# One layer pair of a graph network: who gathers the rows of eight chunks in each edge phase

## The reference, cut to what matters

```python
h = jnp.maximum(_layernorm(x), 0.0)
x = x + attention(h, edge_index, edge_type_3, node_type_3, ...)
# for each of 3 edge types: a weight per edge, exp(leaky_relu(a_s[src] + a_d[dst]) - max per dst),
#   num = segment_sum(w_edge[:, None] * xw[src], dst);  denom = segment_sum(w_edge, dst)
h = jnp.maximum(_layernorm(x), 0.0)
x = x + convolution(h, edge_index, edge_attr_50, ...)
# filters  = silu(edge_attr @ fW1 + fb1) @ fW2 + fb2
# messages = (x[src] @ dW + db) * filters
# aggregated = segment_sum(messages, dst);  then a two-layer update per node
```

## Time and profile before

| | us |
|---|---|
| median of 3 runs (lowest, highest) | 4208.89 (4204.4, 4209.9) |
| span of the profiled execution | 5383.9 |
| busy in it: TensorE, weight loads, VectorE, ScalarE, GpSimd | 3638.4, 2646.4, 2308.2, 1569.4, 3107.3 |

### The profile page before, as it was taken

The page is one execution under the profiler, slowest core; times in us unless marked ns, Lnnn a source line. Parts: engine busy times, 40 slices in busy tenths (PEclk is TensorE's granted clock), DMA queues, the critical chain, the costliest instruction groups (busy, mean ns, idle before and its releaser), DMA issues. The chain is left out here.

```text
span 5383.9 us, 60755 instructions
## 1 busy us (share of the span) xinstructions
PE 3638.4 (68%) x14213; PEld 2646.4 (49%) x14214; DVE 2308.2 (43%) x5525; ACT 1569.4 (29%) x4773; POOL 3107.3 (58%) x3265
## 2 busy tenths in 40 slices
PE   4666666666666666666756767767676777677768
PEld 2444444444444444444545645555455555555556
DVE  5565666565655565655632222222222222222223
ACT  4454444444444444444510100100000000010001
POOL 5565666555655655555455555555555555555553
PEclk6555555555555555555666666666666666566567
DMA  4121222212211211221222222222222222222222
GB/s 103 43 44 42 44 43 45 44 43 43 44 42 42 45 43 42 44 43 43 53 66 59 57 55 59 55 58 59 55 59 53 60 59 54 58 56 57 59 55 57
DMA packets 163399, 280.57 MB, mean 52 GB/s; under 512 B 80268, under 2 KB 105068, under 8 KB 158793
## 3 DMA queue, kind: packets, MB, share of 16 engines
q0 software_dynamic: 102656, 213.73, 17.0%
q1 hardware_dynamic: 60439, 65.39, 4.4%
q10 hardware_dynamic: 200, 0.48, 0.0%
HBM read 268.31 MB, written 9.73 MB: 52 GB/s over the span
## 5 line engine op out<-in xcount | busy, mean ns | idle before, releaser
L60 POOL DMA_INDIRECT ce_xg<-table,ce_idx x1604 | 1519.4, 947 | 1087.9 <-DVE ce_msg L1537 588.0
L60 POOL DMA_INDIRECT ae_xg<-table,ae_idx x1604 | 1521.4, 949 | 1040.0 <-issue 491.4
L1468 PE MATMUL ce_ps_h<-ce_ea,ce_fw 50*128 50x384 f32 x1076 | 654.7, 749 | 481.2 <-ACT ce_hid L1410 313.5
L1410 ACT ACTIVATE ce_hid<-ce_ps_h,ce_fb 128x768 f32<-128x768 f32 x269 | 242.5, 901 | 2378.1 <-remote 1667.5
L808 PE MATMUL ae_ps_k<-ae_xg,ae_e 128*96 128x129 f32 x3224 | 832.3, 431 | 6.9 <-remote 5.8
L1533 DVE TENSOR_TENSOR ce_ring<-ce_ring,ce_fb 128x768 f32<-128x768 f32 x269 | 259.5, 965 | 1292.0 <-remote 883.0
L1447 PEld LDWEIGHTS ce_ring<-ce_fw,ce_hid 128*128 128x128 f32 x3228 | 621.3, 287 | 359.2 <-issue 342.9
L1447 PE MATMUL ce_ring<-ce_fw,ce_hid 128*128 128x128 f32 x3228 | 708.2, 391 | 110.3 <-issue 109.7
L808 PEld LDWEIGHTS ae_ps_k<-ae_xg,ae_e 128*96 128x96 f32 x3224 | 685.2, 277 | 53.0 <-issue 45.5
L1456 PE MATMUL ce_ring<-ce_hot,ce_msg 128*128 128x32 f32 x3224 | 554.2, 324 | 211.4 <-issue 211.0
L1456 PEld LDWEIGHTS ce_ring<-ce_hot,ce_msg 128*128 128x128 f32 x3224 | 570.1, 264 | 201.9 <-issue 201.3
(11 more groups left out here) (156 smaller groups left out, 3278.6 us busy)
## 6 DMA issues: line engine op xcount, KB each, us to landing
ce_ea<-in_edge_attr SPq DMA_DIRECT2D x90, 450.0 KB
ae_xg<-table,ae_idx POOLq DMA_INDIRECT x1604
ce_xg<-table,ce_idx POOLq DMA_INDIRECT x1604
ae_stage<-table SPq DMA_DIRECT2D x1024, 0.5 KB
ce_stage<-table SPq DMA_DIRECT2D x1024, 0.5 KB
sums<-in_x SPq DMA_DIRECT2D x7, 448.0 KB, 4.2
table<-sums SPq DMA_DIRECT2D x6, 462.0 KB, 3.7
fa_x<-in_x SPq DMA_DIRECT2D x6, 448.0 KB, 6.4
```

Of the source, the lines that this page charges most:

```text
L60: eng.indirect_dma_start(out=out, out_offset=None, in_=table[:, :], in_offset=bass.IndirectOffsetOnAxis(ap=idx, axis=0)).then_inc(done, 16)
L1410: nc.scalar.activation(hid[:, b, :].rearrange("p (k e) -> p k e", k=2), ps_h[:, :].rearrange("p (k e) -> p k e", k=2)[:, :, 0:H], ACT.Silu ...
L1468: last = nc.tensor.matmul(ps_h[:, k * 512:k * 512 + H], fw1[:, :], ea[:, s // LOAD, q:q + H], start=True, stop=True)
```

## The change

In both edge phases SyncE no longer gathers rows. `Carry` is gone, with its two staging tiles, its three semaphores for each phase, the index rows kept in `den`, the turn structure `carry_turns` and the input `src_rows`. GpSimd gathers all six chunks of every full unit (four in the last), 1612 in each phase, and its loop is the same as that of the other engines (`turns`: the first turn, a loop over 43, the last). `load_indices` only loads index lists, and attributes in the convolution. VectorE waits for `gathered[s]` alone.

```diff
-def landed_by(r, i, s, carried=0, j=0):
-    if s != CARRY_SLOT:
-        return r * 16 * CH * (TURNS - 1 if s >= REST else TURNS) + 16 * CH * (i + 1)
-    gathers = CH * TURNS - (CH - REST_CH) - CARRIED
-    if isinstance(carried, int):
-        return r * 16 * gathers + 16 * CH * i + 16 * (chunks_of(i, s) - carried)
-    return r * 16 * gathers + 16 * (SPAN * CH - 1) * carried + 16 * CH * j + 16 * CH
+def landed_by(r, i, s):
+    if s < REST - 1:
+        return r * 16 * CH * TURNS + 16 * CH * (i + 1)
+    if s == REST - 1:
+        return r * 16 * (CH * (TURNS - 1) + REST_CH) + 16 * CH * i + 16 * chunks_of(i, s)
+    return r * 16 * CH * (TURNS - 1) + 16 * CH * (i + 1)
...
-class Carry:
...
 def load_indices(...):
...
-        span(r, 0, 0, True)
-        with sp.Fori(0, CARRIED // 2 - 1) as p:
-            span(r, 2 * p + 1, 1)
-            span(r, 2 * p + 2, 0)
-        span(r, CARRIED - 1, 1)
...
+        with sp.Fori(0, TURNS - 1) as i:
+            for v in range(LOADS):
+                read(r, i, v)
+                sp.dma_start(idx[v][:, :], a["src"][...]).then_inc(idx_in[v], 16)
+                ahead(r, i + 1, v)
...
 def gather_units(...):
...
                 pool.wait_ge(xg_free, r * UNITS + (XS if first else i * SL + s + 1))
                 pool.sem_inc(pool_turn, 1)
-                taken = carried is not None and s == CARRY_SLOT
-                for c in range(CH - 1 if taken else chunks_of(i, s)):
+                for c in range(chunks_of(i, s)):
                     k = s % LOAD * CH + c
                     gather(pool, xg[:, s, c, 0:width], table, idx[s // LOAD][:, k:k + 1], gathered[s])
-        turn(0, True, SL)
-        with pool.Fori(1, SPAN) as i:
-            turn(i, False, SL)
-        with pool.Fori(1, SPANS - 1) as t:
-            turn(SPAN * t, False, SL, t)
-            with pool.Fori(1, SPAN) as j:
-                turn(SPAN * t + j, False, SL)
-        turn(SPAN * CARRIED, False, SL, CARRIED)
-        with pool.Fori(SPAN * CARRIED + 1, TURNS - 1) as i:
-            turn(i, False, SL)
-        turn(TURNS - 1, False, REST)
+        turns(pool, turn)
...
-                def messages(n, s, i, carried, j=0):
+                def messages(n, s, i):
...
-                    carry.landed(dve, r, s, carried)
-                    dve.wait_ge(gathered[s], landed_by(r, i, s, carried, j))
+                    dve.wait_ge(gathered[s], landed_by(r, i, s))
```

More of the change, by code:

```diff
@@ L490, in turns @@
     body(TURNS - 1, False, REST)
[L493 to L497, removed]
 def slot(unit):
@@ L570, in load_indices @@
-def load_indices(nc, sp, a, h, idx, idx_in, gathered, landed, carry, table, xg, xg_free, ahead=lambda r, i, v: None):
+def load_indices(nc, sp, a, h, idx, idx_in, gathered, landed, ahead=lambda r, i, v: None):
     def read(r, i, v, count=SL):
         s = min(v * LOAD + LOAD, count) - 1
[L575 to L605, removed]
@@ L606, in load_indices @@
+        sp.wait_ge(gathered[s], landed_by(r, i, s))
     passes = pass_count(sp, h)
@@ L609, in load_indices @@
             ahead(r, 0, v)
-        span(r, 0, 0, True)
-        with sp.Fori(0, CARRIED // 2 - 1) as p:
-            span(r, 2 * p + 1, 1)
-            span(r, 2 * p + 2, 0)
-        span(r, CARRIED - 1, 1)
[L615 to L619, removed]
+        with sp.Fori(0, TURNS - 1) as i:
+            for v in range(LOADS):
+                read(r, i, v)
+                sp.dma_start(idx[v][:, :],
+                             a["src"][bass.ds((i + 1) * LOADS + v, 1), :, 0:P // 2, :].rearrange("u o p c -> (u o) p c")).then_inc(idx_in[v], 16)
+                ahead(r, i + 1, v)
         for v in range(LOADS):
@@ L624, in load_indices, with gather_units, turn @@
         sp.wait_ge(idx_in[v], 16 * (passes * TURNS + 1))
-    sp.wait_ge(carry.list_in, 16 * (passes * CARRIED + 1))
     sp.sem_inc(landed, 1)
-def gather_units(pool, passes, table, xg, width, idx, idx_in, gathered, xg_free, pool_turn, carry):
+def gather_units(pool, passes, table, xg, width, idx, idx_in, gathered, xg_free, pool_turn):
     with pool.Fori(0, passes) as r:
-        def turn(i, first, count, carried=None):
+        def turn(i, first, count):
             for s in range(count):
@@ L711, in _ @@
             project.load(sp, a)
-            load_indices(nc, sp, a, h, idx, idx_in, gathered, landed, carry, table, xg, s_sum)
+            load_indices(nc, sp, a, h, idx, idx_in, gathered, landed)
             sp.wait_ge(merged, 1)
@@ L720, in _ @@
         def _(pool):
-            gather_units(pool, project.pool_passes, table, xg, ROW, idx, idx_in, gathered, s_sum, pool_turn, carry)
+            gather_units(pool, project.pool_passes, table, xg, ROW, idx, idx_in, gathered, s_sum, pool_turn)
         @block.scalar
@@ L892, in types, with score @@
                                             h.iota[:, 0:NT].unsqueeze(1).to_broadcast([P, CH, NT]), ALU.is_equal).then_inc(s_oh, 1)
-                def score(n, s, i, carried, j):
-                    carry.landed(dve, r, s, carried)
-                    dve.wait_ge(gathered[s], landed_by(r, i, s, carried, j))
+                def score(n, s, i):
+                    dve.wait_ge(gathered[s], landed_by(r, i, s))
                     dve.wait_ge(s_oh, n)
@@ L955, in add_sums, with step @@
                     nc.vector.tensor_tensor(state[64:65, :, win], state[64:65, :, win], kv(ps_a[64:65, KEYS:2 * KEYS]), ALU.add).then_inc(s_den, 1)
-                def step(n, s, i, unit, base, stages, fresh, carried=None, j=0, late=0):
+                def step(n, s, i, unit, base, stages, fresh, late=0):
                     look, chain, weigh, rescaled, merge = (k in stages for k in range(5))
@@ L964, in step @@
                         types(unit)
-                        score(n, s, i, carried, j)
+                        score(n, s, i)
                     if weigh:
@@ L979, in step, with turn @@
                         highest(n - 1, s - 1)
-                def turn(i, first, count, carried, j=0):
+                def turn(i, first, count):
                     back = 0 if first else 4
@@ L985, in turn @@
                         step(r * UNITS + i * SL + s + 1, s, i, i * SL + s, lambda k: base[s + back - k],
-                             [k for k in range(5) if not first or k <= s], first, carried, j)
+                             [k for k in range(5) if not first or k <= s], first)
                 start_pass(nc, dve, h, r, steps, key_ready, begun, project.ring, typ, less_key[:, :, :])
                 dve.wait_ge(project.moved, 16 * (NT + 1))
-                carry_turns(dve, turn)
+                turns(dve, turn)
                 base = bases(nc, mybir.EngineType.DVE, h, UNITS - 4, 4)
@@ L1430, in _ @@
         def _(pool):
[L1431 removed]
+            gather_units(pool, project.pool_passes, table, xg, D, sources.idx, sources.idx_in, gathered, s_msg, pool_turn)
         @block.tensor
@@ L1555, in turn @@
                             one_hot(i * SL + s - 1, v)
-                            messages(n - 1, v, i if s else i - 1, carried, j)
+                            messages(n - 1, v, i if s else i - 1)
                 start_pass(nc, dve, h, r, steps, key_ready, begun, ring)
-                carry_turns(dve, turn)
+                turns(dve, turn)
                 n = (r + 1) * UNITS
@@ L1563, in _ @@
                 one_hot(UNITS - 1, slot(UNITS - 1))
-                messages(n, slot(UNITS - 1), TURNS - 1, CARRIED)
+                messages(n, slot(UNITS - 1), TURNS - 1)
                 for k in range(1, 4):
@@ L1647 @@
     arrays["src"] = np.pad(src.reshape(NU // LOAD, 2, P // 2, LOAD * CH), ((0, 0), (0, 0), (0, 1), (0, 0)))
-    carried = (SPAN * SL * np.arange(1, SPANS) + CARRY_SLOT) * CH + CH - 1
-    arrays["src_rows"] = padded(given["src"], EP, 0).reshape(NU * CH, P)[np.append(carried, carried[0])]
     arrays["dst"] = by_unit(given["dst"], N).transpose(1, 0, 2)
```

18 lines of the change are left out of this document (2 added, 16 removed).

## The result

| | before | changed |
|---|---|---|
| median of 4 runs (lowest, highest), us | 4209.4 (4204.4, 4210.69) | 4227.19 (4226.42, 4230.4) |
| ratio, 95% interval | | 1.0047 (1.0035 to 1.0059) |

By the medians the change costs 17.8 us, 0.42%; the ratio, 0.47%, puts it at 19.8 us (14.7 to 24.8). The forecast was 20.0 us, 0.48%, and 4228.9 us, so the median is 1.7 us under it and inside the range of 4214 to 4236 us.

What follows compares the result with a forecast made beforehand. GpSimd's back-to-back gathers were taken as the bound: 60.5 + 2009.8 + 99.2 + 2005.3 + 36.0 = 4210.8 us against a 4208.9 us median. Adding 20.0 us for 16 gathers to that median gave 4228.9 us, range 4214 to 4236.

Steps and rivals of the forecast that it cites:

- The bound: Both edge phases: GpSimd gathers back to back when timed, with at most some 10 us of waits; rebuilt time 4210.8 us.
- The cause of the stalls: The recorded phases' extra 538.6 and 591.4 us were taken for the cost of recording, absent when timed.
- The price: GpSimd in both phases: 8 more gathers each, one pitch of 1.253 or 1.250 us apiece, 20.0 us slower.
- SyncE's part at nothing: SyncE's row issues, list loads and copies are covered by GpSimd's gathers, so dropping them gives 0.
- VectorE's wait for the staged chunk at nothing: In the 16 carried units this wait ends before the one behind it, so losing it gives 0.
- The room under GpSimd: Compute chains take 6.98 us a unit in attention and 7.20 in convolution, under GpSimd's 7.51.
- Rival A: Compute chains end the phases, so no change: 4208.9 us, chance 0.09; in one phase only, 4218.9 us, chance 0.08.
- the rule beside it: Starting transfers from several engines saves only usually small starting time, so dropping SyncE's chunks costs next to nothing.
- Rival B: SyncE's rows delay index lists; removing 25.4 us of GpSimd's list waits makes it faster, 4203.5 us, chance 0.06.
- Rival C: The sixth gather of a carried unit costs more than a pitch: 23.5 us in all, 4232.4 us, chance 0.07.

Runs made afterwards that it cites:

- e4_again: The kernel before, unchanged, recorded a second time: 4209.46 us, with a recorded span of 4207.7 us.
- e1_flat: The changed kernel run again without edit, beside the kernel before on the same chip: 4229.93 against 4210.27 us, ratio 1.0047.
- e5_att_only: The kernel before with the change in the convolution edges only (1604 attention gathers, 1612 convolution): 4225.45 us, ratio 1.0019.
- e7_span3: The kernel before with SyncE gathering a chunk every third turn, not every fifth, leaving GpSimd 1598 a phase: 4201.44 us, ratio 0.996.
- e8_gather5: The changed kernel with five gathers per unit after the first turn, 1350 a phase: 3818.99 us, ratio 0.9053 against the kernel before.
- e2_left_out: The kernel before without SyncE's rows, copies and waits, its eight chunks a phase gathered by nobody: 4210.0 us, ratio 0.9996.
- e3_rows_too: The kernel before with GpSimd gathering all 1612 a phase, SyncE's rows kept but copied to an unread tile: 4230.65 us, ratio 1.0047.
- e6_conv_only: The kernel before with the change in the attention edges only (1612 attention gathers, 1604 convolution): 4224.74 us, ratio 1.0019.

## Why the prediction was right

**The bound.** Right. The whole prediction rested on taking some 1130 us of GpSimd's recorded waits for absent in the timed runs, and on rebuilding the time without them. The second recording of the same kernel shows them absent. Term by term, forecast and e4_again: attention 2009.8 and 2005.18, gap 99.2 and 100.52, convolution 2005.3 and 2009.22, tail 36.0 and 31.90 us; up to the first gather 60.5 and 60.88. The sum was 4210.8 us against a span of 4207.7, for which that run's time was 4209.46. That it came so near is in part luck: its terms are off by +4.6, -1.3, -3.9 and +4.1 us, which mostly cancel. Each is small beside the 1130 us in question, so the conclusion does not hang on it. The same sum with 16 gathers more, 4230.8 us, is 3.6 us over the new median, inside the 5 us that the prediction asked for.

**The cause of the stalls.** Only half right. I took them for the cost of recording and pointed at SyncE's irregular issues. They came in one recording and were gone in the next with the same instructions, so they are not what SyncE's instructions do to a recording. What stopped the engines there is open; no run here tells. The prediction also passed over a large row. Of the 538.6 us that the attention was longer, it named TensorE's 301.2 and called the rest smaller, but GpSimd also has

```profile
POOL ae_xg L60 <- remote: 247.4, 101, 3.8
```

in it: for almost half of the excess no engine of the kernel is named. The second recording has no such wait, so the reading (absent when timed) stands.

**The price.** Right within the interval: 20.0 us forecast, 17.8 and 19.7 us measured by the medians, 19.8 by either ratio. The direction and, within the intervals, the proportion to the count of gathers are shown over the range from 1598 to 1612 a phase: 12 fewer gathers -14.9 us (forecast -15.0), 8 more in one phase +9.1 and +8.4 (10.0), 16 more +17.8 and +19.7 (20.0). The increases lie on the low side by the medians, by no more than the intervals allow. The recordings of the first chip give two small reasons. With SyncE's part held equal, 16 gathers cost 19.0 and 19.1 us and not 20.0; the 0.06 us a gather between 1.19 and the mean pitch has no cause shown. And there SyncE's rows had made each gather some 0.001 us slower, 3.65 us over both phases, so that the phases of e1_flat are only 15.4 us longer than e4_again's. I had put this second effect at 0 and kept 5 us for it in the range; on the second chip it shows in the attention alone. Of the 17.7 us between those spans another 2.6 us lie in the gap between the phases (103.11 and 100.52 us), for which I have no cause. The gap was 100.52, 100.98 and 102.40 us in the three recordings in which SyncE delivers chunks to `xg` in the attention (e4_again, e5_att_only, e7_span3) and 102.74 to 105.42 us in five in which it does not (e8_gather5, where the attention's chain ends the phase, aside). Since e2_left_out (103.52) and e3_rows_too (103.34) are among the five, neither the count of gathers nor the row issues alone set it; this stays open.

**SyncE's part at nothing.** Right for the timed runs: leaving it out gave 0.9996, keeping it beside full gathers gave what e1_flat gave. The cover was GpSimd's half turn of 22.5 us. The estimate of 8.5 us for 13 rows with two list loads was good: in three half turns of e4_again they take 7.3, 9.0 and 9.5 us, from the first list load at 3000.7, 3023.3 and 3045.8 us to the end of the last row at 3008.03, 3032.29 and 3055.26. What the rows may have cost is not time of SyncE but the slower gathers above.

**VectorE's wait for the staged chunk at nothing.** Right: e3_rows_too keeps that wait and has the ratio of e1_flat, which lacks it.

**The room under GpSimd.** Right in sign. For the attention the undisturbed 6.98 us a unit was the floor of a unit and not of the phase: e8_gather5 gives 7.13, so the room is 0.35 us a unit in place of 0.53, and 94 us in place of 143. For the convolution I had 7.20 us a unit from the recorded clock; the phase went to 6.29 us and was still not bound by it. That estimate was too high by at least 0.9 us a unit, because it took the recorded clock as fixed: at the 0.76 granted in e8_gather5 the same working gives 0.48 x 8.12 + 0.52 x 4.28 = 6.12 us.

**Rival A, and the rule beside it.** A falls by e8_gather5 and by the two halves. The Trainium skill (DMA: Bandwidth & Descriptors, Issuing engines are not separate DMA queues) says that issuing from several engines saves only the sequencer's starting time, usually small beside the transfer. The first half agrees with e1_flat against the kernel before: both move the same rows, and what differs is that GpSimd starts 16 gathers more, 1.25 us each, and 19.7 us in the time. The second half does not hold in this kernel: a start takes 1.25 us with its gap, where a gather lands 2.5 us after its issue (median of the changed kernel), and in e4_again 3208 such starts make up 4014 of 4208 us while the DMA engines are busy 0.23 to 0.27 of the time.

**Rival B** (late index lists) falls: in e4_again GpSimd waits for no list, so there was nothing to give back.

**Rival C** (a dearer sixth gather, 23.5 us) is inside the intervals of both timed comparisons (14.7 to 24.8 and 13.9 to 25.7 us). The recordings speak against it: the mean gather is 0.945 us (attention) and 0.946 us (convolution) in the changed kernel, and 16 more cost 19.0 and 19.1 us.

## What to carry to other kernels

Look for the engine that the others wait for, not for the busiest one. Here GpSimd, at 74% busy with gaps that are all the same 0.30 us, was full. TensorE, at 84%, was not the bound: with a sixth of the gathers left out and TensorE's work unchanged, the kernel was 397 us shorter. If a recording is much longer than the timed runs, cut it into stretches, take the pitch from where nobody waits, and see whether the stretches without the waits add up to the measured time before believing any wait in it. On the engine that bounds a phase each instruction is worth its whole pitch, so moving 1 gather in 200 to an idle engine pays as long as the index loads behind it stay on time; SyncE had room for 14 chunks a phase here (0.35% under the kernel before by the medians, 0.40% by the ratio).

## What the runs showed of the hardware

- Two recordings of one kernel on the same program had spans of 5383.9 and 4207.7 us, with equal counts; in the longer one engines stood still for up to some 20 us (ScalarE 21.61 us in the earlier trace rows) with no cause in the trace. The timed runs had nothing of it (4204.4 to 4210.7 us).
- Indirect gathers of 128 rows keep a pitch of 1.249 to 1.255 us over 1350 to 1612 in a row, in every stretch where no slot is waited for, with rows of 528 bytes as with rows of 512. Without SyncE's rows the pitch was 1.249 and 1.251 us in the two phases on one chip (e1_flat) and 1.251 and 1.254 us on another (e6_conv_only's attention, e5_att_only's convolution).
- A row issue by SyncE costs 0.56 to 0.73 us with its registers and its share of the list loads (7.3 to 9.5 us for 13 in e4_again, 14.2 us for 21 in e7_span3), so a chunk of 128 rows is some 70 to 95 us of SyncE, an estimate from these, against 1.25 us of GpSimd; it pays only because SyncE would otherwise wait.
- With five gathers in a unit TensorE's granted clock in the convolution was 0.76 and not 0.66, while its busy share went from 86% (1726.70 of 2009.22 us) to 89% (1513.06 of 1692.14 us).
